# V of two units at once by seven block products, from the second head group on

## The chip, the cores and the metric

The kernel runs on one core of a Trainium2 chip. The metric is the device time in microseconds (us) of one execution. Before the change its median over 3 runs is 834.77 us, from 833.03 to 836.32.

## The reference

A gated cross attention with 32 heads of 128 and then a feed-forward layer with a router and eight low-rank experts, both with a residual. There are 8 batches of 128 tokens with 512 features, and a context of the same shape. Cut to what matters here:

```python
x = rmsnorm(layernorm(x)) * ln_weight
h_q = x @ w_q.T
h_k = ctx @ w_k.T
h_v = ctx @ w_v.T
score = softmax(where(m, einsum(h_q, h_k) + position_bias, -inf))
attn = einsum(score, h_v)
out = attn @ w_out.T
x = x + tanh(g_xattn) * (hidden + out)
x = x + tanh(g_ffn) * ffn(layernorm(x))
```

Everything is float32. A product is made of three TensorE products of the type fp32r: each operand is split into a rounded part (`_hi`) and the rest (`_lo`), and low x high, high x low and high x high are added up in PSUM.

## The kernel before

Two phases and a tail follow one another.

In the first phase 32 jobs make K and then Q of all heads, two heads a job, and store them to DRAM (`qk_units`). From the third job on a job is done by the Winograd form of Strassen's scheme: seven products of blocks in the place of eight, with four sums of weight blocks (S1 to S4, made by VectorE, DVE) and four sums of context blocks (T1 to T4, kept in `t_hi`, `t_lo`).

In the second phase the heads go in 8 groups of 4. A unit is one batch in one group, so there are 64 units, and `step(g, b, q)` is written for each engine. A step of TensorE (PE) is: `scores` of unit t (4 heads, full float32), the first half of V of unit t+1 (`v_half`), the first half of the output projection of unit t-5 (`out_half`), the second halves of both, and `apply_probs` of unit t-3. V of a unit is 12 matmuls of 512 columns: four chunks of the 512 features by the three parts. ScalarE (ACT) copies V out of PSUM (`v_evict`), makes the high parts of the weights and of the attended values, and does the exponentials. GpSimd (POOL) adds bias and mask and makes the low parts of the weights. DVE adds scores and bias, finds the maxima, normalises, transposes 32x32 blocks and adds the projections to `acc`.

All DMAs are issued by SyncE (SP), in the order in which they are written, and they go through one hardware queue. In a step of group g SP does: `store_blocks` (probabilities to DRAM, `p_rows`), `load_unit` (K and Q of a later unit, 512 KB), `load_blocks` (four DMAs back into `pT`, after a wait for the landing of the rows), then one load of 256 KB of weights for a later step. Groups 1 to 6 are a hardware loop of two groups each; group 0 and group 7 are written out. In group 0 `first_units` has the first steps, and `group(0, 0)` goes on from step 4.

Each engine works through its own list in order and waits on semaphores; no planner moves anything.

Of the kernel before, what the change touches and what calls it, by code (L numbers as in the profile page):

```python
# [50 lines left out]

def build(nc, x, ctxT, mask, g_xattn, g_ffn, bias, lnw, wqk, wv, wo, baseT, base_b, loraR, router_b,
          lora_B, expert_map, qk_units, p_rows, out):
    with ExitStack() as ctx:
# [16 lines left out]
        c_hi, c_lo = sb("c_hi", [P, 4, 2, TH], F32R), sb("c_lo", [P, 4, 2, TH], F32R)  # L71
# [31 lines left out]
        with ExitStack() as first_phase:  # L103
# [3 lines left out]
            t_hi, t_lo = sb_a("t_hi", [P, 4, 2, TH], F32R), sb_a("t_lo", [P, 4, 2, TH], F32R)  # L107
# [15 lines left out]
        v_hi1, (v_raw1, v_lo1) = sb("v_hi1", [P, DC, HU * DH], F32R), loaded_and_low("v1", [P, DC, HU * DH])  # L123
        o_hi1, (o_raw1, o_lo1) = sb("o_hi1", [P, HU, D], F32R), loaded_and_low("o1", [P, HU, D])
        hwT_hi, hwT_lo = (sb(n, [P, BH * S], F32R)[:, :] for n in ("hwT_hi", "hwT_lo"))

        y_cols01 = sb("y_cols01", [P, 2, DC, S])
        v_hi0, (v_raw0, v_lo0) = sb("v_hi0", [P, DC, HU * DH], F32R), loaded_and_low("v0", [P, DC, HU * DH])
# [6 lines left out]
        out_more = sb("out_more", [P, D])  # L135
        y_ring = sb("y_ring", [P, 2, D])
        spare = sb("spare", [P, D])

        p_blocks, pT = sb("p_blocks", [P, 2, Q32, HU, 32]), sb("pT", [P, 4, Q32, HU, 32])
        x_again = sb("x_again", [P, 2, D])  # L140
        A_hi, A_lo = sb("A_hi", [P, 2, HU, S], F32R), sb("A_lo", [P, 2, HU, S], F32R)
        y_cols23 = sb("y_cols23", [P, 2, DC, S])
        y_cols = [t[:, k, :, :] for t in (y_cols01, y_cols23) for k in range(2)]

        v_raw, v_hi, v_lo = [v_raw0, v_raw1], [v_hi0, v_hi1], [v_lo0, v_lo1]
        o_raw, o_hi, o_lo = [o_raw0, o_raw1], [o_hi0, o_hi1], [o_lo0, o_lo1]
        picked = spare[:, 0:BH * E * NR].rearrange("p (i e n) -> p i e n", i=BH, e=E)

        base_raw, w_base_hi, w_base_lo = o_raw0, o_hi0, o_lo0
        loraR_all = v_raw0[:, 0:2, :].rearrange("p c n -> p (c n)")[:, 0:DC * RW].rearrange("p (c n) -> p c n", c=DC)  # L150
        loraB_raw, w_loraB_hi, w_loraB_lo = v_raw0[:, 2, :], v_hi0[:, 2, :], v_lo0[:, 2, :]
# [57 lines left out]
        v_done, v_out = sem("v_done"), sem("v_out")  # L209
        o_done, acc_done = sem("o_done"), sem("acc_done")  # L210
# [46 lines left out]

        def x_columns(t, j):
            b = tok(j % BH)
            return t[:, 0:2, :, b].rearrange("p k c n -> p (k c) n") if j < BH else t[:, 2, :, b]  # L260
# [5 lines left out]
        def c_tile(t, j, c):  # L266
            return t[:, 2 * (j // BH) + c // 2, c % 2, tok(j % BH)]
# [11 lines left out]
        def v_bank(t, b):  # L279
            return V_bank[b % 2]  # L280

# [21 lines left out]
        def _(sp):  # L303
# [15 lines left out]
            def load_wv(g, q, k):  # L319
                if k == 0:  # L320
                    reached(sp, v_done, B * (g - 1))
                sp.dma_start(v_raw[q][:, k, :], wv[g, :, k, :]).then_inc(ld_wv[k], 16)

            def load_wo(g, q, k):
                if k == 0:
                    reached(sp, o_done, B * (g - 1))
                sp.dma_start(o_raw[q][:, k, :], wo[g, :, k, :]).then_inc(ld_o[k], 16)
# [20 lines left out]
            def load_unit(g, b):  # L348
                sp.dma_start(qk[:, b % 4, :, :, :].rearrange("p h a k -> p (h a k)"),
                             qk_units[2 * g + b // BH, :, b % BH, :, :].rearrange("p c k -> p (c k)")).then_inc(  # L350
                                 ld_qk[b % 4], 16)
# [19 lines left out]
            for n in range(JOBS + 1):  # L371
# [5 lines left out]
                if n == 19:  # L377
                    for k in range(4):
                        sp.wait_ge(t_lo_done[k], 2)
                    for k in range(DC):  # L380
                        load_wv(0, 0, k)
                    for k in range(HU):
                        load_wo(0, 0, k)
                if n >= JOBS - 2 and n < JOBS:
                    sp.wait_ge(w2_lo, J(n))
                    sp.wait_ge(st[R11], 16 * (G + 2))
                    sp.wait_ge(st[R21], 16 * (G + 2))
# [15 lines left out]
            def first_units():  # L403
# [18 lines left out]
                for k in range(3):  # L422
                    load_wv(1, 1, k)

            def group(g, q):
                first, last = (isinstance(g, int) and g == n for n in (0, GROUPS - 1))
                for b in range(4 if first else 0, B):
# [3 lines left out]
                    before = (g, b - 1) if b > 0 else (g - 1, B - 1)  # L431
                    store_blocks(*before)
# [14 lines left out]
                    if last and b == 0:  # L447
                        for j in range(2):
                            sp.dma_start(x_again[:, j, :], x[:, j, :]).then_inc(ld_x2[j], 16)
                        sp.wait_ge(v_done, LAST)  # L450
                        sp.dma_start(loraR_all, loraR).then_inc(ld_lora, 16)
                        sp.dma_start(loraB_raw, lora_B).then_inc(ld_loraB, 16)
                    if last and b >= 2:
                        sp.wait_ge(f_u, b - 1)
                        sp.dma_start(x_again[:, b % 2, :], x[:, b, :]).then_inc(ld_x2[b % 2], 16)
# [6 lines left out]
            with sp.Fori(0, GROUPS // 2 - 1) as pair:  # L462
                for k in range(2):
                    group(2 * pair + 1 + k, 1 - k)
# [4 lines left out]
            for j in range(B):  # L469
                sp.wait_ge(f_out, j + 1)  # L470
                sp.dma_start(out[:, j, :], out_ring[j % 2]).then_inc(stored[j % 2], 16)
# [4 lines left out]
        def _(pool):  # L476
# [37 lines left out]
            def split_wv_lo(g, q, k):  # L514
# [1204 lines left out]
```

## Time and profile before

| what | value |
|---|---|
| median of 3 runs | 834.77 us |
| span of the profiled execution, first to last instruction | 830.8 us |
| TensorE busy, weight loads busy | 817.8 us (98%), 695.2 us (84%) |
| DVE, ACT, POOL busy | 59%, 52%, 42% |
| the chain that ended last, on TensorE | 95% |
| first step of group 0 to last step of group 7 | 313 to 763 us |

The page gives no other time of the profiled execution than its span; it lies 4.0 us under the median. A busy time counts an instruction from its start to its modelled end, and matmuls overlap: a matmul of 512 columns is shown as 0.39 us long and the next starts 0.23 us after it. So the pace of TensorE is read from starts and not from lengths. Groups of instructions can mix many places in the program, and a line can be that of a helper (L1339 to L1341 are the three parts of every plain product).

### The profile page before, as it was taken

To read this page: it belongs to the slowest core of one execution; us is meant where nothing else is said; L and a number is where in the kernel's file an instruction comes from. 1 tells how busy PE (TensorE), PEld (TensorE's weight loads), DVE (VectorE), ACT (ScalarE), POOL (GpSimd) and SP (SyncE) were. 2 spreads that over 40 slices of the span, in tenths; PEclk is the share of its full clock that TensorE was granted. 3 is DMA by queue.
4 is the path that set the end of the run, shared out by engine and by line. 5 is a ranking of instruction groups with operands and counts; after the bars stand their busy time and mean duration, and the time that the engine had idled before them with its cause. 6 is when DMAs were issued, how large, how long until landed. Compare 5 with 4: busy or idle time off the path is not lost.

```text
span 830.8 us, 13207 instructions
## 1 busy us (share of the span) xinstructions
PE 817.8 (98%) x4172; PEld 695.2 (84%) x4172; DVE 490.8 (59%) x918; ACT 428.9 (52%) x1064; POOL 348.7 (42%) x223
## 2 busy tenths in 40 slices
PE   6999999999999999999999999999999999999998
PEld 5888888888888888888888888888888888888876
DVE  6666666674353335555665565556655655677875
ACT  6567766676676665544444444444444444444320
POOL 0354544564556551434443344344434434432332
PEclk9999999999999999999999999999999999999999
DMA  8655555568555565766665566676665666654002
GB/s 293 208 168 152 162 164 153 165 178 270 171 168 156 172 202 167 238 193 199 192 209 185 180 197 211 185 202 176 185 194 175 178 192 188 219 164 159 33 26 76
DMA packets 147197, 147.58 MB, mean 178 GB/s; under 512 B 10960, under 2 KB 109392, under 8 KB 146768
## 3 DMA queue, kind: packets, MB, share of 16 engines
q1 hardware_dynamic: 147152, 147.02, 58.3%
q8 instruction: 23, 0.38, 0.2%
q14 instruction: 22, 0.18, 0.1%
HBM read 94.55 MB, written 52.43 MB: 177 GB/s over the span
## 4 chain that ended last, share of the span: by engine, by line
PE 95%; DVE 3%; issue 1%; DMA 0%; ACT 0%; SPq 0%; DVEq 0%
PE Sb L1496 7%; PE Ab L1507 7%; PE Sb L1348 7%; PE Sb L1349 7%; PE Sb L1350 7%; PE Vb L1339 4%; PE Vb L1340 4%; PE Vb L1341 4%; PE Kb L1339 4%; PE Kb L1340 4%; PE Kb L1341 4%; PE Ob L1339 4%; PE Ob L1340 4%; PE Ob L1341 4%; PE Ab L1348 3%; PE Ab L1349 3%
## 5 line engine op out<-in xcount | busy, mean ns | idle before, releaser
L530 POOL TENSOR_TENSOR bm<-bias,maskneg 128x512 f32<-128x512 f32 x64 | 83.7, 1307 | 178.1 <-DVE s_sb L1064 178.1
L750 ACT ACTIVATE p_exp<-s_sb,negmax 128x128 f32<-128x128 f32 x256 | 99.8, 391 | 77.0 <-DVE negmax L1066 77.0
L493 POOL TENSOR_TENSOR w_lo<-w_raw,w_hi 128x1280 fp32r<-128x1280 f32 (+1 forms) x29 | 86.9, 2996 | 117.7 <-ACT w_hi L620 117.7
L620 ACT ACTIVATE A_hi<-Ab 128x512 fp32r<-128x512 f32 x64 | 38.3, 598 | 163.6 <-PE Ab L1507 163.6
L1064 DVE TENSOR_TENSOR s_sb<-Sb,bm 128x512 f32<-128x512 f32 x62 | 42.8, 691 | 122.8 <-PE Sb L1496 122.8
L620 ACT ACTIVATE U<-Sb 128x512 f32<-128x512 f32 x90 | 53.9, 599 | 65.9 <-PE Sb L1350 65.3
L521 POOL TENSOR_TENSOR o_lo<-o_raw,o_hi 128x512 fp32r<-128x512 f32 x32 | 52.5, 1641 | 45.0 <-ACT o_hi L620 45.0
L1507 PEld LDWEIGHTS Ab<-pT,V 128*128 128x128 f32 x512 | 66.9, 191 | 5.0
L620 ACT ACTIVATE w_hi<-w_raw 128x512 fp32r<-128x512 f32 (+2 forms) x67 | 60.0, 900 | 21.2 <-PE Kb L1350 8.5
L1348 PE MATMUL Sb<-t_hi,w_lo 128*128 128x512 f32 x180 | 70.1, 389 | 0.0
L1350 PE MATMUL Sb<-t_hi,w_hi 128*128 128x512 f32 x180 | 70.0, 389 | 0.0
L1349 PE MATMUL Sb<-t_lo,w_hi 128*128 128x512 f32 x180 | 70.0, 389 | 0.0
L516 POOL TENSOR_TENSOR v_lo<-v_raw,v_hi 128x512 fp32r<-128x512 f32 x32 | 51.5, 1612 | 42.2 <-ACT v_hi L620 42.2
L1507 PE MATMUL Ab<-pT,V 128*128 128x128 f32 x512 | 67.3, 274 | 0.0
L1496 PE MATMUL Sb<-qk 128*128 128x128 f32 x496 | 65.5, 275 | 0.0
L1496 PEld LDWEIGHTS Sb<-qk 128*128 128x128 f32 x496 | 60.6, 192 | 0.2
L498 POOL TENSOR_TENSOR w_lo<-w_raw,w_hi 128x512 fp32r<-128x512 f32 x30 | 40.6, 1353 | 37.8 <-ACT w_hi L620 37.7
L1339 PE MATMUL Vb<-v_hi,c_lo 128*128 128x512 f32 x128 | 52.6, 411 | 0.0
L1339 PE MATMUL Kb<-v_hi,c_lo 128*128 128x512 f32 x128 | 52.5, 410 | 0.0
L1087 DVE STREAM_TRANSPOSE p_blocks<-p_norm 128x512 f32<-128x512 f32 x64 | 45.5, 711 | 10.0 <-DVE p_norm L1081 8.3
L1339 PE MATMUL Ob<-o_hi,A_lo 128*128 128x512 f32 x128 | 50.1, 392 | 0.2 <-DVE A_lo L917 0.2
L1340 PE MATMUL Kb<-v_lo,c_hi 128*128 128x512 f32 x128 | 50.0, 391 | 0.0
(276 smaller groups left out, 2090.0 us busy)
## 6 DMA issues: line engine op xcount, KB each, us to landing
qk_units<-unit_out SPq DMA_DIRECT2D x128, 256.0 KB, 2.9
qk<-qk_units SPq DMA_DIRECT2D x64, 512.0 KB, 4.8
p_rows<-p_blocks SPq DMA_DIRECT2D x64, 256.0 KB, 2.7
pT<-p_rows SPq DMA_DIRECT2D x256, 64.0 KB, 2.7
w_raw<-wqk SPq DMA_DIRECT2D x31, 512.0 KB, 4.0
v_raw<-wv SPq DMA_DIRECT2D x32, 256.0 KB, 4.1
o_raw<-wo SPq DMA_DIRECT2D x32, 256.0 KB, 3.9
stage<-ctxT SPq DMA_DIRECT2D x8, 256.0 KB, 5.9
```

Of the source, the lines that this page charges most:

```text
L493: pool.tensor_tensor(w_lo[:, n % 2, first:5, :], w_raw[:, n % 2, first:5, :], f32(w_hi[:, n % 2, first:5, :]), ALU.subtract).then_inc(w1_l ...
L530: pool.tensor_tensor(bm[:, :, :], bias4[:, q, :, :], maskneg[:, b:b + 1, :].broadcast_to([P, HU, S]), ALU.add).then_inc(bm_done, 1)
L620: act.activation(dst, src, ACT.Copy).then_inc(done, 1)
L750: last = act.activation(p_exp[:, i, :], s_sb[:, i, :], ACT.Exp, bias=negmax[:, i:i + 1], accum_out=rowsum[:, i:i + 1])
L1339: pe.matmul(dst, w_lo, m_hi, start=start, stop=False)
L1340: pe.matmul(dst, w_hi, m_lo, start=False, stop=False)
L1341: return pe.matmul(dst, w_hi, m_hi, start=False, stop=stop)
L1348: pe.matmul(bank, lo, m_hi[:, c, :], start=first, stop=False, skip_group_check=not fresh)
L1349: pe.matmul(bank, hi, m_lo[:, c, :], start=False, stop=False, skip_group_check=not fresh)
L1350: last = pe.matmul(bank, hi, m_hi[:, c, :], start=False, stop=c == 1, skip_group_check=not fresh)
L1496: last = pe.matmul(s_bank(u, b)[:, h, :], qk[:, b % 4, h, 1, :], qk[:, b % 4, h, 0, :], start=True, stop=True)
L1507: last = pe.matmul(a_bank(b)[:, h, :].rearrange("p (i r) -> p i r", i=Q32), V[:, b, h, :], pT[:, b % 4, :, h, :], start=True, stop=True)
```

## The change

From group 1 on V is made for two units together, those of batch p and batch p + 4. Their 256 tokens by 512 features, and the 512 x 512 weights of the group, are cut into 2 x 2 blocks (128 tokens, 256 features, 256 columns), and the same Winograd form as in the first phase is used: seven block products, each of 2 chunks by 3 parts = 6 matmuls of 256 columns. So a pair of units takes 42 matmuls of 256 columns, where it took 24 of 512. The sums of context blocks are those of the first phase: SP stores T1 to T4 to DRAM (`ctx_sums`, eight DMAs of 512 KB) in jobs 4 to 7, and reads them back in group 0, since Q's sums overwrite them. Batches go in the order 0, 4, 1, 5, 2, 6, 3, 7. Group 0 makes V as before.

Further parts: ACT takes three copies of 256 columns out of PSUM for a pair and writes one quarter of V; DVE adds the other three quarters, and makes four sums of weight blocks a group; the seven blocks of the weights are split (ACT high, POOL low) in steps 5 to 7 of the group ahead, where four whole chunks were split in steps 3 to 6. The loads of the weights move to steps 2 and 3, two a step, and those of the output weights to step 7 and steps 0 to 2. Group 1 and group 6 are written out, and the loop is one turn shorter.

```diff
-            def v_half(u, g, b, q, k):
+            def v_blocks(dst, i, a, m_hi, m_lo, fresh, done):
+                hi, lo = v_block_hi[a], v_block_lo[a]
+                for c in range(2):
+                    first = fresh and c == 0
+                    pe.matmul(dst, m_lo[:, c, tok(i)], hi[:, c, :], start=first, stop=False, skip_group_check=not fresh)
+                    pe.matmul(dst, m_hi[:, c, tok(i)], lo[:, c, :], start=False, stop=False, skip_group_check=not fresh)
+                    last = pe.matmul(dst, m_hi[:, c, tok(i)], hi[:, c, :], start=False, stop=c == 1,
+                                     skip_group_check=not fresh)
+                last.then_inc(done, 1)
...
+            def vm6(g, i):
+                v_split_reached(g, i, 1)
+                if isinstance(g, int) and g == 1 and i == 0:
+                    pe.wait_ge(ld_t[T2], SUM_LOADED)
+                pe.wait_ge(vu_done, 3 * v_job(g, i) + 1)
+                v_blocks(VX, i, S2, t_hi[:, T2, :, :], t_lo[:, T2, :, :], False, vm_done[6])
...
+            def v_part(g, b, k):
+                first, last = (isinstance(g, int) and g == n for n in (0, GROUPS - 1))
+                job = (g + 1, 0) if b == B - 1 else (g, (b + 1) // 2)
+                ends = last and b == B - 1
+                if first and b < B - 1:
+                    v_half(b + 1, k)
+                elif b % 2 == 1 and k == 0:
+                    if not ends:
+                        vm1(*job)
+                    if not first:
+                        vm3(g, b // 2)
+                elif b % 2 == 1:
+                    if not ends:
+                        vm6(*job)
+                        vm2(*job)
+                elif k == 0:
+                    vm7(*job)
+                    vm5(*job)
+                else:
+                    vm4(*job)
...
                 if not (first and b < 5):
                     out_half(*before, 1)
+                if first and b == B - 1:
+                    for k in (T3, T1, T4):
+                        pe.wait_ge(ld_t[k], SUM_LOADED)
                 apply_probs(t - 3, *((g, b - 3) if b >= 3 else (g - 1, b + 5)))
...
+            def load_context_sum(k):
+                for part, t in enumerate((t_hi, t_lo)):
+                    sp.dma_start(f32(t[:, k, :, :]), ctx_sums[k, part, :, :, :]).then_inc(ld_t[k], 16)
...
-                for k in range(3):
-                    load_wv(1, 1, k)
+                for k in (RAW_A21, RAW_A22, RAW_A11, RAW_A12):
+                    load_wv(1, k)
+                load_context_sum(T2)
...
-                    if 1 <= b <= 4 and not last:
-                        load_wv(g + 1, 1 - q, b - 1)
-                    if b >= 5 and not last:
-                        load_wo(g + 1, 1 - q, b - 5)
-                    if b == 0:
-                        load_wo(g, q, 3)
+                    if 2 <= b <= 3 and not first and not last:
+                        for k in ((RAW_A21, RAW_A22), (RAW_A11, RAW_A12))[b - 2]:
+                            load_wv(g + 1, k)
+                    if first and b < 7:
+                        load_context_sum((T3, T1, T4)[b - 4])
+                    if b == 7 and not last:
+                        load_wo(g + 1, 1 - q, 0)
+                    if b < 3 and not first:
+                        load_wo(g, q, b + 1)
```

The first place is TensorE in the last step of group 0, where the second half of V follows the first half of the output projection (`Vb`, `Kb`, `Ob`, `Ab`, `Sb` are PSUM banks). Before:

```order
L1339 MATMUL Ob<-o_hi0,A_lo 128x512
L1340 MATMUL Ob<-o0_lo,A_hi 128x512
L1341 MATMUL Ob<-o_hi0,A_hi 128x512
L1339 MATMUL Vb<-v_hi1,c_lo 128x512
L1340 MATMUL Vb<-v1_lo,c_hi 128x512
L1341 MATMUL Vb<-v_hi1,c_hi 128x512
```

Now, with the first product that reads a loaded context sum (`ld_xA` is the semaphore of T2's loads, `vu_done` that of ACT's copies):

```order
L1541 MATMUL Ob<-o_hi0,A_lo 128x512
L1542 MATMUL Ob<-o0_lo,A_hi 128x512
L1543 MATMUL Ob<-o_hi0,A_hi 128x512
L1669 MATMUL Vb<-va_hi,t_lo 128x256 [waits vu_done,ld_xA,w2_lo]
L1670 MATMUL Vb<-va_lo,t_hi 128x256
L1671 MATMUL Vb<-va_hi,t_hi 128x256
```

Matmuls of 256 columns stand in the place of those of 512, and the product waits for ACT and for a load. The end of the same step in the changed kernel, and the beginning of group 1 (`ld_xB`, `ld_w0a` and `ld_w0b` are the semaphores of T3, T1 and T4):

```order
L1541 MATMUL Ob<-o_hi0,A_lo 128x512
L1542 MATMUL Ob<-o0_lo,A_hi 128x512
L1543 MATMUL Ob<-o_hi0,A_hi 128x512
L1790 MATMUL Ab<-pT,V 128x128 [waits pt_done0,v_out,ld_w0b,a_lo_done,ld_w0a,ld_xB]
L1790 MATMUL Ab<-pT,V 128x128 x3
L1775 MATMUL Sb<-qk 128x128 [waits s_done,ld_qk0]
L1775 MATMUL Sb<-qk 128x128 x3
L1669 MATMUL Vb<-v_hi0,t_lo 128x256 [waits vu_done,w2_lo]
```

`apply_probs` of this one step stands behind the landing of three context sums; before, it waited for its probabilities, V and a buffer alone.

The second place is SP in group 0, from the weights of group 1 on. Before:

```order
L322 DMA v_raw<-wv 128x512 [waits m4_done]
L322 DMA v_raw<-wv 128x512 x2
L335 DMA p_rows<-p_blocks 128x512 [waits blocks_done,pt_done1]
L349 DMA qk<-qk_units 128x1024 [waits scores_done]
L341 DMA pT<-p_rows 32x4x128 [waits rows_done]
L341 DMA pT<-p_rows 32x4x128 x3
L322 DMA v_raw<-wv 128x512
L346 DMA bias<-bias 128x512
```

Now:

```order
L403 DMA v_raw<-wv 128x512 [waits m4_done]
L403 DMA v_raw<-wv 128x512 x3
L417 DMA t_hi<-ctx_sums 128x1024
L417 DMA t_lo<-ctx_sums 128x1024
L425 DMA p_rows<-p_blocks 128x512 [waits blocks_done,pt_done1]
L440 DMA qk<-qk_units 128x1024 [waits scores_done]
L431 DMA pT<-p_rows 32x4x128 [waits rows_done]
L431 DMA pT<-p_rows 32x4x128 x3
L417 DMA t_hi<-ctx_sums 128x1024
L417 DMA t_lo<-ctx_sums 128x1024
L436 DMA bias4<-bias 128x512
```

One more load of weights and the two parts of T2 stand ahead of the rows of step 4, and the two parts of T3 stand in the place of one load of weights; in steps 5 and 6 T1 and T4 stand in the same way where a load of output weights (L327) stood.

## Rows read from the trace of the kernel before

**Rows 1.** The page: span, busy time of each engine, the chain by engine.
```profile
span 830.8 us, 13207 instructions
PE 817.8 (98%) x4172; PEld 695.2 (84%) x4172; DVE 490.8 (59%) x918; ACT 428.9 (52%) x1064; POOL 348.7 (42%) x223
PE 95%; DVE 3%; issue 1%; DMA 0%; ACT 0%; SPq 0%; DVEq 0%
```

**Rows 2.** Windows, second phase: busy us (x instructions) by engine; clock; DMA share, GB/s.
```profile
500.00:550.00 50.00, 50.00 (x279) 43.48 (x278) 29.59 (x56) 22.57 (x77) 20.57 (x14) 1.00 0.63 190
```

**Rows 3.** Timeline of TensorE, one step: start, length (us), line, out<-in, count.
```profile
502.11 1.06 PE L1496 MATMUL Sb<-qk 128*128 128x128 f32 x8
...
503.24 0.40 PE L1340 MATMUL Vb<-v_lo,c_hi 128*128 128x512 f32 x1
...
508.23 0.39 PE L1341 MATMUL Ob<-o_hi,A_hi 128*128 128x512 f32 x1
508.46 1.05 PE L1507 MATMUL Ab<-pT,V 128*128 128x128 f32 x8
509.35 1.06 PE L1496 MATMUL Sb<-qk 128*128 128x128 f32 x8
```

**Rows 4.** Timeline of all engines, same step: weight loads (PEld) where V begins.
```profile
502.89 0.19 PEld L1339 LDWEIGHTS Vb<-v_hi,c_lo 128*128 128x128 f32 x1
...
503.01 0.19 PEld L1340 LDWEIGHTS Vb<-v_lo,c_hi 128*128 128x128 f32 x1
```

**Rows 5.** Timeline of TensorE in the tail: eight full float32 matmuls of 144 columns.
```profile
780.99 1.15 PE L1532 MATMUL Sb<-v_raw,y_cols 128*128 128x144 f32 x8
...
782.21 0.40 PE L1340 MATMUL Ob<-o_lo,A_hi 128*128 128x512 f32 x1
```

**Rows 6.** Timeline of TensorE at the start, after its longest idle time.
```profile
6.85 0.77 PE L1339 MATMUL Sb<-c_hi,w_lo 128*128 128x512 f32 x1 [6.85 <-DVE c_lo L917]
...
7.84 0.63 PE L1341 MATMUL Sb<-c_hi,w_hi 128*128 128x512 f32 x1
8.27 0.63 PE L1339 MATMUL Sb<-c_hi,w_lo 128*128 128x512 f32 x1
...
10.06 0.39 PE L1340 MATMUL Sb<-c_lo,w_hi 128*128 128x512 f32 x1
```

**Rows 7.** Timeline of SP in group 0: issue time, length of issuing, line, DMA, count.
```profile
336.62 0.43 SPq L349 DMA_DIRECT2D qk<-qk_units  x1
...
338.57 0.38 SPq L335 DMA_DIRECT2D p_rows<-p_blocks  x1
...
344.41 1.92 SPq L341 DMA_DIRECT2D pT<-p_rows  x4
346.37 0.43 SPq L322 DMA_DIRECT2D v_raw<-wv  x1
...
353.34 1.75 SPq L341 DMA_DIRECT2D pT<-p_rows  x4
355.13 0.43 SPq L327 DMA_DIRECT2D o_raw<-wo  x1
...
360.08 1.74 SPq L341 DMA_DIRECT2D pT<-p_rows  x4
361.86 0.43 SPq L327 DMA_DIRECT2D o_raw<-wo  x1
```

**Rows 8.** Windows of 2 us in group 0, columns as in Rows 2: DMA at its fullest.
```profile
328.00:330.00 2.00, 2.00 (x15) 1.79 (x14) 0.44 (x1) 1.49 (x6) 1.09 (x1) 1.00 0.98 268
350.00:352.00 2.00, 2.00 (x16) 1.83 (x15) 0.67 (x1) 1.60 (x3) 0.92 (x1) 1.00 1.10 377
```

**Rows 9.** DMA issues of the whole run: KB of one, median us from issue to landing.
```profile
o_raw<-baseT SPq DMA_DIRECT2D x1, 1024.0 KB, 6.2
```

**Rows 10.** Timeline of TensorE: `apply_probs` that ends the last step of group 0.
```profile
363.66 1.05 PE L1507 MATMUL Ab<-pT,V 128*128 128x128 f32 x8
```

**Rows 11.** Groups of the steady stretch (372 to 748 us): busy us, mean ns of one.
```profile
L516 POOL TENSOR_TENSOR v_lo<-v_raw,v_hi 128x512 fp32r<-128x512 f32 x24 | 40.5, 1686 | 39.0 <-ACT v_hi L620 39.0
L620 ACT ACTIVATE v_hi<-v_raw 128x512 fp32r<-128x512 f32 x25 | 15.4, 616 | 0.0
```

More of the change, by code:

```diff
@@ L141, in build @@
         A_hi, A_lo = sb("A_hi", [P, 2, HU, S], F32R), sb("A_lo", [P, 2, HU, S], F32R)
[L142 to L146, printed above, removed]
+        with ExitStack() as tail:
+            w_loraB_hi = tail.enter_context(nc.sbuf_tensor("w_loraB_hi", [P, D], F32R))[:, :]
@@ L256, in J, with y_tiles, v_tile @@
             return n + 1 - PLAIN
+        def y_tiles(t, t2, j):
+            return (t if j < BH else t2)[:, 0:2, :, tok(j % BH)]
+        def v_tile(of, j, c):
+            half, i = j % 2, j // 2
+            return of(2 * half + c // 2)[:, c % 2, tok(i)]
         def x_columns(t, j):
@@ L431, in group @@
                     before = (g, b - 1) if b > 0 else (g - 1, B - 1)
+                    if b == 2 and not first and not last:
+                        sp.wait_ge(v_lo_done, PRODUCTS + 7 * g)
                     store_blocks(*before)
@@ L461, in _ @@
             group(0, 0)
-            with sp.Fori(0, GROUPS // 2 - 1) as pair:
+            group(1, 1)
+            with sp.Fori(0, GROUPS // 2 - 2) as pair:
                 for k in range(2):
-                    group(2 * pair + 1 + k, 1 - k)
+                    group(2 * pair + 2 + k, k)
+            group(GROUPS - 2, 0)
             group(GROUPS - 1, 1)
@@ L587, in _ @@
                 step(0, b, 0)
-            with pool.Fori(0, GROUPS // 2 - 1) as pair:
+            for b in range(B):
+                step(1, b, 1)
+            with pool.Fori(0, GROUPS // 2 - 2) as pair:
                 for k in range(2):
                     for b in range(B):
-                        step(2 * pair + 1 + k, b, 1 - k)
-            for b in range(B):
-                step(GROUPS - 1, b, 1)
+                        step(2 * pair + 2 + k, b, k)
+            for k in range(2):
+                for b in range(B):
+                    step(GROUPS - 2 + k, b, k)
             def base_low(k):
@@ L1130, in step @@
                 first, last = (isinstance(g, int) and g == n for n in (0, GROUPS - 1))
+                job = (g + 1, 0) if b == B - 1 else (g, (b + 1) // 2)
+                strassen = not (first and b < B - 1) and not (last and b == B - 1)
                 if first and b == 6:
@@ L1134, in step @@
                 attention_lo(t - 4, b % 2)
+                if b % 2 == 1 and not first:
+                    v_c12(g, b // 2)
+                if strassen and b % 2 == 0:
+                    v_c22(*job)
+                if not last and b == 7:
+                    weight_sum(g + 1, S4)
                 if last and b >= 6:
@@ L1143, in step @@
                     x1(2)
+                if strassen and b % 2 == 1:
+                    v_c11(*job)
                 normalise(t, b)
                 transpose_blocks(t, b)
+                if not last and 4 <= b <= 5:
+                    for a in ((S1,), (S3, S2))[b - 4]:
+                        weight_sum(g + 1, a)
                 if last and b == 6:
@@ L1238, in _ @@
                 step(0, b, 0)
-            with dve.Fori(0, GROUPS // 2 - 1) as pair:
+            for b in range(B):
+                step(1, b, 1)
+            with dve.Fori(0, GROUPS // 2 - 2) as pair:
                 for k in range(2):
                     for b in range(B):
-                        step(2 * pair + 1 + k, b, 1 - k)
-            for b in range(B):
-                step(GROUPS - 1, b, 1)
+                        step(2 * pair + 2 + k, b, k)
+            for k in range(2):
+                for b in range(B):
+                    step(GROUPS - 2 + k, b, k)
             def logits(h):
@@ L1537, in step @@
                 t = B * g + b
-                first, last = (isinstance(g, int) and g == n for n in (0, GROUPS - 1))
+                first = isinstance(g, int) and g == 0
                 before = (t - 5, g, b - 5, q) if b >= 5 else (t - 5, g - 1, b + 3, 1 - q)
-                after = (t + 1, g, b + 1, q) if b < B - 1 else (t + 1, g + 1, 0, 1 - q)
-                ends = last and b == B - 1
                 scores(t, g, b)
-                if not ends:
-                    v_half(*after, 0)
+                v_part(g, b, 0)
                 if not (first and b < 5):
                     out_half(*before, 0)
-                if not ends:
-                    v_half(*after, 1)
+                v_part(g, b, 1)
                 if not (first and b < 5):
                     out_half(*before, 1)
+                if first and b == B - 1:
+                    for k in (T3, T1, T4):
+                        pe.wait_ge(ld_t[k], SUM_LOADED)
                 apply_probs(t - 3, *((g, b - 3) if b >= 3 else (g - 1, b + 5)))
```

400 lines of the change are left out of this document (285 added, 115 removed).

## Prediction

> **What bounds the kernel now.** I read the page first: the chain that ended last lies on TensorE for 95%, and TensorE is busy for 98% of the span [rows 1]. Then the windows of the second phase: TensorE is busy in all 50 of 50 us there at the clock's upper level (2.4 GHz, granted share 1.00), while DVE has 29.6, ACT 22.6 and POOL 20.6 us of work, and DMA a share of 0.63 [rows 2]. Then the timeline of TensorE for one step: it lasts 509.35 - 502.11 = 7.24 us with no gap in it [rows 3]. So in this phase a column saved on TensorE is time saved, until something else is late. What one matmul costs is read from starts: from 503.24 to 508.23 there are 22 matmuls of 512 columns, 0.2268 us each; a full float32 product of 128 columns shows as two records, and eight of them take 508.46 to 509.35, 0.111 us each [rows 3].
>
> **What is saved on TensorE.** V of a pair of units is 24 x 0.2268 = 5.443 us now, and will be 42 matmuls of 256 columns; 28 pairs change (7 groups of 4). No row shows an fp32r matmul of 256 columns, so its pace is bounded.
> From below: the 128-column float32 records take 0.111 us each, with a weight load for each; 256 columns at 2.4 GHz are 0.1067 us, so each record takes about as long as 256 columns would. Those of 144 columns take (782.21 - 0.227 - 780.99) / 8 = 0.124 us [rows 5], so these records grow with their columns and nothing holds them above that. For fp32r weights, one load starts at 502.89 and the next at 503.01, 0.12 us later [rows 4].
> From above: 512 columns at 2.4 GHz are 0.2133 us, and the matmul takes 0.0135 us more. If that excess belongs to each matmul, 256 columns take 0.1067 + 0.0135 = 0.120 us; if it belongs to the columns, half of 0.2268, 0.113 us. At the lower clock level 512 columns take 8.27 - 7.84 = 0.43 us, which is 512 / 1.2 GHz with no excess [rows 6], so the trace does not tell the two apart.
> I take the middle of the last two, 0.117 us: 42 x 0.117 = 4.914 us a pair, 0.529 us less. **28 x 0.529 = 14.8 us saved**; 11.3 us at 0.120, 19.0 at 0.113, 21.9 at 0.111. The change breaks even on TensorE at 5.443 / 42 = 0.1296 us.
>
> The weight loads grow by 28 x 18 = 504, 0.19 us each as the rows show them, some 96 us on the 695 us that they are busy [rows 1, 4]. The Trainium skill (Perfetto Trace Analysis, Identifying the Most-Contended Engine) takes the busy share of weight loads as the measure of what TensorE has left; by it, 791 us of loads in about 830 would leave almost nothing, and this change would gain little. But the two loads in rows 4 begin 0.12 us apart and are 0.19 us long each: they overlap, and here the measure overstates.
>
> **What it costs: the context sums in group 0.** T1 to T4 come back through SP's one queue, 1024 KB each, between rows that others wait for. SP waits for the landing of a step's probabilities before it goes on. In the trace, the rows issued at 338.57 have landed by 344.41, and those of the next steps by 353.34 and 360.08; the output weights that T4 replaces are issued at 361.86 [rows 7]. I move T4's issue by the bytes put ahead of it. Ahead of the first rows: 256 KB of weights and T2, 1.31 MB. Ahead of the second: T3 for 256 KB of weights (346.37), 0.79 MB more. Ahead of the third: T1 for 256 KB of output weights (355.13), 0.79 MB more. The queue at its fullest moves 377 GB/s, DMA share over 1 [rows 8]: 3.5 + 2.1 + 2.1 = 7.7 us. So T4 is issued at 361.86 + 7.7 = 369.6. A DMA of 1024 KB lands after 6.2 us [rows 9], and T4 is two issues, 0.5 us apart: it lands at 376.3.
> TensorE waits for it before the last `apply_probs` of group 0. That starts at 363.66 now [rows 10]; with 18 matmuls of 256 columns in that step (2.11 us) for 12 of 512 (2.72 us), at 363.05. **So TensorE stands for 13.2 us.** ACT splits the first weight blocks only when V of group 0 is through, which may hold TensorE for some us earlier in this step; that falls into the same wait. After its longest idle time so far, 6.85 us, TensorE ran at the lower level: seven starts from 6.85 to 10.06 took 3.21 us, not 1.59 [rows 6]. I add **1.6 us** for the same after this wait.
> Bounds: at 268 GB/s, which another full window shows [rows 8], the 2.89 MB take 10.8 us, and the wait is 16.3 us. If they delayed nothing, T4 would be issued at 361.86 and the wait would still be 5.5 us.
>
> **What costs nothing, and its cover.** ACT's three copies out of PSUM: each is at most the 0.62 us of 512 columns [rows 11]; M6 follows M1 by half an output projection and, mostly, another product (1.36 + 0.70 us), M7 follows M6 by over 3 us, and M4 follows M7 by 2 us. Without that cover a late copy costs TensorE its lateness, 28 times. DVE gets three adds a pair and four sums a group, each under 0.7 us, on a load of 59% [rows 1]: about 75%. M2 waits for an add that comes some 0.9 us sooner, the tightest of them. POOL's low parts, 1.69 us each [rows 11], stand three, three and one in steps 5 to 7; the first is wanted in step 7, some 7 us after it is done. The output weights now land one step before ACT splits them instead of three; ACT has about 2 us of slack there. The eight stores in jobs 4 to 7 add 1 MB to a job of some 10 us; weights are loaded a job ahead. The order of batches moves nothing in time. The tail has the same products and frees its loads earlier: I count 0.
>
> **The sum.** Against the profiled span: 830.8 - 14.8 + 13.2 + 1.6 = 830.8; the median lies 4.0 us over that span, so 834.8 us.
>
> **Rivals.** *The gain wins (faster).* Matmuls of 256 columns run as the 128-column float32 records do, 0.111 us: 21.9 us saved, 14.8 lost, 827.7 us. For it: nothing in rows 3 to 5 forces more. Against it: the only fp32r row carries an excess of 0.0135 us. The Trainium skill (TensorE: Matmul & The Clock Gate, Back-to-back issue gap) gives 262 cycles for 256 columns, 0.109 us; by it 24.1 us would be saved and the time would be 825.5 us. The trace speaks against its figure for 512 columns, 518 cycles or 0.216 us, with 0.2268 us.
> *T4 does not hold TensorE.* If queue and landings are quicker than the rows suggest, or the wait is covered, 834.8 - 14.8 = 820 us. Against it: even undelayed, T4 lands 5.5 us late.
> *The loads of group 0 cost more than the products save (slower).* Place: the queue of SP from 337 to 380 us. Price: at 268 GB/s 16.3 + 1.6 = 17.9 us; with the excess per matmul, 11.3 us saved: 841.4 us. It decides from 377 us for T4's landing at 0.120 us a matmul, and from 380 us at 0.117. For it: window 328 to 330 is full at 268 GB/s. Against it: the window of the very place shows 377.
> *A new wait in every group.* ACT waits for the output weights, copies late, and TensorE stands 1 us a group: 7 us, 842 us. SP is the engine whose rows come late by some us in places.
> *Weight loads do not overlap for short matmuls.* At 0.19 us each a pair takes 7.98 us, 28 x 2.54 = 71 us more, 920 us. Rows 4 speak against it.
>
> **How the numbers follow.** Forecast 0.42; faster by the matmul's pace 0.27; T4 no hindrance 0.05; slower by the loads 0.18; by a new wait 0.05; by weight loads 0.03. Half a per cent, 4.2 us, is about what a measurement of this kernel can tell from no change. Faster by more: 0.27 + 0.05 = 0.32; within: 0.42; slower: 0.18 + 0.05 + 0.03 = 0.26. The range takes in 827.7 us, somewhat less wait with it, and both slower cases about 842: 825 to 842 us. Outside are T4 without hindrance, the serial loads, and part of the ends, together under 0.2. The forecast's own range is 831 to 839 us.
>
> **What would show it.** In the timeline of the changed kernel, starts of 256-column matmuls in V: 0.117 us apart (over 0.13 and the change loses). A pair of steps: 14.48 us now, 13.95 after. In group 0, an idle time of TensorE of about 13 us ahead of the last `apply_probs`, ended by the DMA of a context sum near 376 us, and starts 0.43 us apart behind it. No other idle time of TensorE between there and the tail. The prediction is wrong if that wait is under 9 us or over 17, or if TensorE stands in every group.

## The result and the profile after

The changed kernel takes **846.61 us** (median of 4 runs, 845.49 to 848.5), the kernel before 835.21 beside it: a ratio of 1.0155, interval 1.0142 to 1.0168. It is slower, above the range of the prediction. The profiled span grew from 830.8 to 843.7 us, by 12.9.

The first lines of the page of the changed kernel (of before: [rows 1]), with its second part's line of the granted clock and the packets of the instruction queue:

```profile
span 843.7 us, 14600 instructions
...
PE 815.0 (97%) x4676; PEld 713.0 (85%) x4676; DVE 568.8 (67%) x1030; ACT 453.5 (54%) x1141; POOL 355.7 (42%) x244
...
PEclk9999999999999999979999999999999999999999
...
q8 instruction: 41, 0.67, 0.3%
...
PE 88%; DVE 6%; issue 3%; ACT 2%; DMA 0%; DVEq 0%; ACTq 0%; SPq 0%
```

In what follows M1 to M7 are the seven block products of a pair of units: M6 multiplies S2 and T2, M7 S3 and T3, and M4 a block of the weights and T4. TensorE has 504 more matmuls and is busy for 2.8 us less, but 28.7 us of the span are now idle (13.0 before), and the chain lies on it for 88%, where it was 95% [rows 1]. The windows tell where (columns as in [rows 2]):

```profile
350.00:400.00 50.00, 39.15 (x248) 35.47 (x247) 29.12 (x50) 20.99 (x67) 19.85 (x16) 0.90 0.76 242
...
500.00:550.00 50.00, 48.75 (x333) 44.51 (x332) 39.89 (x71) 25.97 (x87) 22.15 (x17) 1.00 0.62 187
550.00:600.00 50.00, 47.87 (x320) 44.07 (x320) 34.64 (x63) 21.47 (x73) 14.79 (x12) 0.97 0.59 178
```

Two places stand out by idle time and by a granted clock under 1: the end of group 0, and the stretch around 550 us. Between them a little is missing, as from 500 to 550 us. Before, TensorE was busy in all of each of these ([rows 2] for the second of the three), as two more windows of that kernel show:

```profile
350.00:400.00 50.00, 50.00 (x277) 43.36 (x276) 30.23 (x56) 22.83 (x77) 21.41 (x15) 1.00 0.65 203
...
550.00:600.00 50.00, 50.00 (x279) 43.48 (x278) 30.04 (x55) 22.14 (x76) 20.93 (x14) 1.00 0.63 185
```

The waits of TensorE in the changed kernel from 300 to 400 us (total, times, longest), and the two largest from 395 to 775 us:

```profile
PE Ab L1790 <- issue: 9.0, 1, 9.0
PE Vb L1669 <- ACT VU L726: 1.9, 1, 1.9
```
```profile
PE Sb L1775 <- issue: 2.8, 1, 2.8
PE Vb L1669 <- ACT VU L726: 2.2, 6, 0.4
```

The four, in the order of the kernel:

**Group 0.** The timeline of TensorE around the last `apply_probs` of group 0 [rows 10]:

```profile
362.25 0.36 PE L1669 MATMUL Vb<-va_hi,t_lo 128*128 128x256 f32 x1 [1.86 <-ACT VU L726]
...
374.29 2.05 PE L1790 MATMUL Ab<-pT,V 128*128 128x128 f32 x8 [8.99 <-issue]
376.13 1.91 PE L1775 MATMUL Sb<-qk 128*128 128x128 f32 x8
```

M6 waits 1.9 us for ACT, and `apply_probs` 9.0 us. For the second wait the profile names no releaser ("issue"). It is put down to T4 by SP's timeline (of before: [rows 7]), and experiments 1 and 7 bear that out:

```profile
359.75 0.43 SPq L417 DMA_DIRECT2D t_hi<-ctx_sums  x1
...
368.44 0.43 SPq L417 DMA_DIRECT2D t_hi<-ctx_sums  x1
368.92 0.43 SPq L417 DMA_DIRECT2D t_lo<-ctx_sums  x1
```

T4 is issued at 368.44 and 368.92. Its second part lands 5.2 us after its issue, at 374.1, and TensorE goes on at 374.29, at the clock's lower level: `apply_probs` and the scores behind it show 2.05 and 1.91 us in the place of 1.05.

**The pace of 256 columns.** One stretch of the steady state, TensorE's timeline:

```profile
485.68 0.28 PE L1669 MATMUL Kb<-v_hi,cs_lo 128*128 128x256 f32 x1
...
486.40 0.40 PE L1541 MATMUL Ob<-o_hi,A_lo 128*128 128x512 f32 x1
...
487.78 0.28 PE L1669 MATMUL Vb<-va_hi,t_lo 128*128 128x256 f32 x1
```

Six starts from 485.68 to 486.40 are 0.120 us each. The six of 512 columns behind them take 1.38 us, 0.230 each, where it was 0.2268 [rows 3].

**A wait in six groups.** In step 6 of groups 1 to 6 M7 starts late. The timelines of ACT and of TensorE in group 1:

```profile
421.79 0.63 ACT L726 ACTIVATE va_hi<-v_raw 128x512 fp32r<-128x512 f32 x1 [4.07 <-DVE v_raw L1257]
...
422.85 0.58 ACT L726 ACTIVATE A_hi<-Ab 128x512 fp32r<-128x512 f32 x1
423.32 0.38 ACT L726 ACTIVATE VU<-Vb 128x256 f32<-128x256 f32 x1
```
```profile
423.10 0.39 PE L1543 MATMUL QP<-o_hi1a,A_hi 128*128 128x512 f32 x1
423.75 0.38 PE L1669 MATMUL Vb<-v_hi,t_lo 128*128 128x256 f32 x1 [0.26 <-ACT VU L726]
```

ACT stands 4.07 us before the high part of S2, a sum of weight blocks that DVE makes, and behind it in ACT's list come the copy of the attended values and the copy out of PSUM that M7 needs. M7 starts 0.65 us after the matmul ahead of it, not 0.23.

**The loop's way back.** Group 4 begins with the second turn of the loop:

```profile
548.12 1.05 PE L1790 MATMUL Ab<-pT,V 128*128 128x128 f32 x8
551.97 1.59 PE L1775 MATMUL Sb<-qk 128*128 128x128 f32 x8 [2.80 <-issue]
...
553.58 0.41 PE L1670 MATMUL Vb<-v_lo,t_hi 128*128 128x256 f32 x1
553.79 0.41 PE L1671 MATMUL Vb<-v_hi,t_hi 128*128 128x256 f32 x1
```

Nothing that the profile shows is waited for ("issue"), and the matmuls behind it are 0.21 us apart, the lower clock level.

**The ledger**, from the starts of the steps. Undisturbed, a step with 18 block matmuls lasts 6.71 us and one with 24 lasts 7.43: 14.14 a pair, 14.48 before. Steps 7 to 62 are 29 of the first kind and 27 of the second, 395.2 us, against 56 x 7.24 = 405.4: 10.2 us saved. Lost in the same steps: 13.4 in steps 7 and 8 (19.0 and 7.79 us), 4.2 in step 6 of six groups and behind it, 5.0 in steps 31 and 32 (10.54 and 8.64 us). The second phase begins 0.2 earlier; from step 63 on it takes 0.9 longer, 0.7 of it M3 of the last pair, which was moved there. -10.2 + 22.6 - 0.2 + 0.9 = 13.1; the spans give 12.9.

### The profile page after: what moved, and what is told of

It reads as the page before. It is cut to its first block, busy times and chain, and to the rows that moved or that the text cites. A ratio compares the mean times of both kernels' runs of the same rounds, so it can differ in the third digit from the quotient of the medians.

```text
span 843.7 us, 14600 instructions
## 1 busy us (share of the span) xinstructions
PE 815.0 (97%) x4676; PEld 713.0 (85%) x4676; DVE 568.8 (67%) x1030; ACT 453.5 (54%) x1141; POOL 355.7 (42%) x244
## 4 chain that ended last, share of the span: by engine, by line
PE 88%; DVE 6%; issue 3%; ACT 2%; DMA 0%; DVEq 0%; ACTq 0%; SPq 0%
PE Sb L1550 6%; PE Sb L1552 6%; PE Sb L1551 6%; PE Sb L1775 6%; PE Ab L1790 6%; PE Ob L1541 3%; PE Ob L1542 3%; PE Ob L1543 3%; PE Ab L1552 3%; PE Ab L1550 3%; PE Ab L1551 3%; PE Vb L1669 3%; PE Vb L1670 3%; PE Vb L1671 3%; PE QP L1541 3%
## 5 line engine op out<-in xcount | busy, mean ns | idle before, releaser
L726 ACT ACTIVATE VU<-Vb 128x256 f32<-128x256 f32 x84 | 32.1, 382 | 64.4 <-PE Vb L1671 64.3
L1228 DVE TENSOR_TENSOR p_norm<-p_exp,rscale 128x512 f32<-128x512 f32 x64 | 52.4, 819 | 2.2
L1064 DVE TENSOR_TENSOR A_lo<-Ab,A_hi 128x512 fp32r<-128x512 f32 x64 | 43.6, 681 | 7.1 <-ACT A_hi L726 7.1
L871 ACT ACTIVATION_READ_ACCUMULATOR p_exp<-s_sb,negmax 128x1 f32 x256 | 48.0, 188 | 0.0
L1213 DVE TENSOR_REDUCE negmax<-s_sb 128x4 f32<-128x512 f32 x64 | 43.9, 686 | 2.2
L789 ACT ACTIVATE unit_out<-Ob 128x512 f32<-128x512 f32 x61 | 36.4, 596 | 12.5 <-DVE Ob L1125 8.7
```

The costliest lines, as they stand in the source:

```text
L726: act.activation(dst, src, ACT.Copy).then_inc(done, 1)
L871: last = act.activation(p_exp[:, i, :], s_sb[:, i, :], ACT.Exp, bias=negmax[:, i:i + 1], accum_out=rowsum[:, i:i + 1])
L1228: dve.tensor_tensor(p_norm[:, :, :], p_exp[:, :, :], scale, ALU.mult).then_inc(norm_done, 1)
```

## The experiments

**1. Without the context sums' loads.** The loads are left out, so the first sums of Q's contexts take their place and V is not the reference's.

```diff
-        SUM_LOADED = 16 + 32
+        SUM_LOADED = 16
...
             def load_context_sum(k):
-                for part, t in enumerate((t_hi, t_lo)):
-                    sp.dma_start(f32(t[:, k, :, :]), ctx_sums[k, part, :, :, :]).then_inc(ld_t[k], 16)
+                return
```

> The changed kernel without the eight loads of context sums in group 0; the stores stay. V is then made with the sums of Q that lie in the tiles, so its values are not the reference's; the work on the engines is the same. Theory (the queue of SP in group 0 holds TensorE): the wait of 9.1 us before the last apply_probs of group 0 goes, and the slow starts behind it; the 2.0 us before M6, which ACT causes, stay. 846.6 - 9.1 - 1.3 = 836 us. Rival (ACT's split of the weights, which waits for V of group 0, is the real hold, and the wait only moves): 843 us or more.

Measured: 836.18 us, ratio 1.0018 (1.0002 to 1.0034), 11.4 us under the changed kernel by the ratios (their difference times 834.5 us, as in what follows). The loads cost that much. One wait is left from 300 to 400 us:

```profile
PE Vb L1668 <- ACT VU L725: 1.9, 1, 1.9
```

So M6's wait does not come from the loads. By the code and ACT's order, ACT holds the first weight blocks of group 1 until V of group 0 is through, and M6 waits for a copy behind them.

**2 and 3. The loop written out**, in the changed kernel and in the one before (the same edit, one turn more).

```diff
-            with pe.Fori(0, GROUPS // 2 - 2) as pair:
+            for pair in range(GROUPS // 2 - 2):
...
```

> The changed kernel with all groups written out, no hardware loop. Theory (the loop's one way back costs 3.1 us of instruction fetching in TensorE's queue and 1.9 us of slow starts behind it): 846.6 - 5.0 = 841.6 us, and no idle time of TensorE between step 31 and step 32. Rival (written-out code costs as much, since instructions are fetched all the time): 846.6 us, with waits spread over the groups.

> The kernel before with all groups written out. In its trace no instruction is fetched while the loop runs, and its steps at the loop's two ways back last 7.24 us like all others. Theory (the way back is free as long as the body stays in the fetch buffer, and written-out code is fetched ahead): 835.2 us, no change. Rival (written-out code costs): over 837 us.

Measured: 842.11 us, ratio 1.0094 (1.0073 to 1.0116), for the changed kernel; 834.56 us, 1.0001 (0.9989 to 1.0013), for the one before. The way back costs the new loop some 5 us and the old one nothing.

**4. Half columns alone.** The kernel before, all groups written out, with each matmul of V of 512 columns as two of 256: 768 matmuls more, no block products, no sums, no new waits. Its V is not the reference's.

```diff
-                for c in (2 * k, 2 * k + 1):
-                    made = product(v_bank(u, b), ...)
+                for r in range(2):
+                    cols = slice(2 * DH * r, 2 * DH * (r + 1))
+                    for c in (2 * k, 2 * k + 1):
+                        ... three matmuls into v_bank(u, b)[:, cols]
```

> The kernel before, written out, with each of the 12 matmuls of V of a unit split into two of 256 columns: the same columns, twice the matmuls, and none of the sums, copies and waits of the change. At 0.120 us each V of a unit takes 24 x 0.120 = 2.88 us in the place of 12 x 0.2268 = 2.72, 64 x 0.158 = 10.1 us more than before_written_out: 845 us. If the 512-column matmuls of the output projection also slow down behind short ones, as they do in the changed kernel (0.231 us in the place of 0.227), 64 x 12 x 0.0045 = 3.5 us more: 849 us. If that slowing comes from the other engines' new work, 845 us stays.

Measured: 845.33 us, ratio 1.0127 (1.0104 to 1.015). By the time alone that is the 845 us of an unchanged projection and not the 849 of a slower one; what tells them apart is the pace in its timeline:

```profile
505.69 0.28 PE L1461 MATMUL Kb<-v_lo,c_hi 128*128 128x256 f32 x1
505.81 0.28 PE L1462 MATMUL Kb<-v_hi,c_hi 128*128 128x256 f32 x1
505.94 0.40 PE L1339 MATMUL QP<-o_hi,A_lo 128*128 128x512 f32 x1
506.17 0.40 PE L1340 MATMUL QP<-o_lo,A_hi 128*128 128x512 f32 x1
```

0.12 us again, and 0.23 for the output projection behind them. A step lasts 7.43 us, not 7.24: 12 matmuls more at 0.0133 us are 0.16, the rest goes with the 12 of the projection. So the excess of some 0.013 us belongs to each matmul, at 256 columns as at 512, and the slower projection comes with the short matmuls and not with the block products' adds and copies. Why it is slower stays open.

**5. The same, in the loop.** The kernel before with its loop of three turns, and V's matmuls halved as in 4 (and V as there).

> The kernel before with its loop kept, in which each matmul of V of 512 columns is two of 256 (as in before_half_columns, whose groups are all written out; V's values are not the reference's here either, since the second half's sum begins in the same bank). TensorE's part of the loop grows from 16 x 32 = 512 matmuls to 16 x 44 = 704; in the changed kernel it has 16 x 41 = 656. Theory: the 5 us that the changed kernel loses at its loop's way back come from the size of the loop's body, so this loop of three turns loses them at both of its ways back: 845.3 + 2 x 5 = 855 us, with an idle time of TensorE of some 3 us and slow starts behind it at each. Rival: they come from something else in the changed kernel (its semaphores, another engine's late turn); the ways back stay free, and it takes 845.3 us as with all groups written out.

Measured: 852.11 us, ratio 1.0204 (1.0185 to 1.0223); 6.4 us over the written-out one by the ratios, where 10 were expected and the rival had none. TensorE's waits from 300 to 775 us, and the timeline at the first way back:

```profile
PE Sb L1501 <- issue: 4.8, 2, 2.5
```
```profile
486.73 1.40 PE L1501 MATMUL Sb<-qk 128*128 128x128 f32 x8 [2.25 <-issue]
487.79 0.56 PE L1460 MATMUL Kb<-v_hi,c_lo 128*128 128x256 f32 x1
488.14 0.41 PE L1461 MATMUL Kb<-v_lo,c_hi 128*128 128x256 f32 x1
```

The two steps at each way back last 4.0 and 4.3 us longer than two undisturbed ones, with the same wait and the same slow starts (8.3 us; the second phase of this execution began 1.6 us earlier). So the loss comes with the size of TensorE's part of the loop: free with 512 matmuls, not with 656 or 704. That a larger body must be fetched again fits the instruction queue: 23 packets in the kernel before, 41 after, 44 here. From 475 to 711 us, through both of its ways back, the kernel before fetches none, while the changed one fetches in its second turn too. The fetching itself was not tried, so the reason stays an inference.

**6. The weight sums one step earlier**, in each group that makes block products.

```diff
-                if not last and 4 <= b <= 5:
-                    for a in ((S1,), (S3, S2))[b - 4]:
+                at = 4 if first else 3
+                if not last and at <= b <= at + 1:
+                    for a in ((S1,), (S3, S2))[b - at]:
```

> The changed kernel, with VectorE's three sums of context tiles one step earlier in every group from the second on (S1 in step 3, S3 and S2 in step 4), the first group as it is. Theory: the wait of TensorE before the seventh block product in step 6 of each of the seven groups (0.5 to 0.7 us each) comes from the sum S2 on VectorE by way of ScalarE's copy of its high part, so it goes: steps 14, 22, 30 and so on last 6.71 us, and the time is 846.6 - 4 = 842.5 us. Rival: the wait comes from ScalarE's own queue, whatever the sums do; the steps stay at 7.2 to 7.4 us and the time at 846.6.

Measured: 843.12 us, ratio 1.0102 (1.0082 to 1.0122), 4.4 us lower by the ratios. Every step 6 now lasts 6.71 us, and from 395 to 775 us one wait is left:

```profile
PE Sb L1776 <- issue: 2.9, 1, 2.9
```

**7. Each sum waited for where it is read.** The waits for T3, T1 and T4 leave `apply_probs` and go to M7, M5 and M4 of the first pair.

```diff
-                if first and b == B - 1:
-                    for k in (T3, T1, T4):
-                        pe.wait_ge(ld_t[k], SUM_LOADED)
...
+                if isinstance(g, int) and g == 1 and i == 0:
+                    pe.wait_ge(ld_t[T4], SUM_LOADED)
```

> The changed kernel, in which TensorE waits for T3, T1 and T4 not before the last scores product of the first group but each at the block product that reads it (T3 and T1 in the first half of step 8, T4 in its second). Theory: T4 lands at 374.1 us as before, and the 3.7 us of step 8's work ahead of the product that reads it go in front of the wait: 9.1 us of wait become 5.4, and the time is 846.6 - 4 = 842.6. Rival: TensorE's later steps wait for the same landing by another way, and it stays at 846.

Measured: 844.38 us, ratio 1.0119 (1.01 to 1.0138), 3 us lower by the ratios, where 4 were expected. From 300 to 400 us:

```profile
PE Vb L1669 <- issue: 3.6, 1, 3.6
PE Vb L1669 <- ACT VU L726: 3.3, 2, 1.9
```

9.0 us at one place became 3.6, with another wait of 1.5 us for ACT behind it.

**8. The sums loaded earlier in SP's queue**, and ACT's first three blocks without the wait for V of group 0.

```diff
                 load_blocks(0, 0)
+                sp.wait_ge(m_done[4], J(JOBS - 1))
+                load_context_sum(T2)
...
                 load_blocks(0, 1)
+                load_context_sum(T3)
...
-                    if first and b < 7:
-                        load_context_sum((T3, T1, T4)[b - 4])
+                    if first and b == 4:
+                        load_context_sum(T4)
...
-                    act.wait_ge(v_done, B)
+                    if n >= 3:
+                        act.wait_ge(v_done, B)
```

> The changed kernel with the four context sums of the first group loaded earlier (T2 and T3 right behind the first two block loads of the second phase, T1 behind a load of the V weights, T4 at step 4 instead of 6), and ScalarE's copy of V's high part in the second group without the wait for the first group's last V. Theory: both waits of step 7 (2 us before the sixth product, 9 us before the last scores product) and the slow starts behind them go: step 7 lasts 6.7 to 7.4 us, and the time is 846.6 - 12.5 = 834 us. Rival: the block loads and the weights are pushed back by the same 4 MB, and TensorE stands earlier in the group, for 5 to 10 us: 840 to 846 us.

Measured: 842.37 us, ratio 1.0088 (1.0064 to 1.0112). By the ratios 5.6 us of the 12.5 went, and the time is the rival's. The four runs lie between 839.68 and 847.55 us, and the trace is that of 847.55. From 340 to 400 us:

```profile
PE Vb L1672 <- ACT VU L728: 6.7, 2, 5.5
PE Ab L1793 <- DMA pT<-p_rows: 2.9, 2, 1.7
```

The sums are there. In steps 6 and 7 the probabilities come late, and with them what ACT does in order: 4.1 us of these waits. SP's timeline has the reason:

```profile
347.15 0.64 SPq L417 DMA_DIRECT2D t_lo<-ctx_sums  x1
347.89 0.53 SPq L425 DMA_DIRECT2D p_rows<-p_blocks  x1
...
356.54 1.74 SPq L431 DMA_DIRECT2D pT<-p_rows  x4
```

From the issue of step 4's 256 KB of probabilities until SP goes on with them 8.6 us pass, behind weights and a sum (5.8 before, [rows 7]). The longest wait, 5.5 us in step 9, has another releaser. ACT stands before an output weight, which SP issues at 381.75, and the copy that M6 needs comes behind it; ACT's timeline:

```profile
386.06 0.63 ACT L728 ACTIVATE o_hi1a<-o1a_raw 128x512 fp32r<-128x512 f32 x1 [9.93 <-DMA o1a_raw<-wo]
```

**9. Edits 2, 6 and 8 together.**

> The changed kernel with all groups written out, VectorE's sums one step earlier, and the context sums loaded earlier. Theory: the three costs (12.5 us of the first group, 5 us of the way back of the loop, 4 us of the sums) add up and all go, so that what is left is the gain of the block products at 0.120 us each: 56 steps in pairs of 14.14 us instead of 14.48; 846.6 - 21.5 = 825 us, 1.2% faster than the kernel before. Rival: they cover each other, and one of them stays: 830 to 835 us.

Measured: 833.65 us, ratio 1.0001 (0.9982 to 1.002): no difference from the kernel before, 9 us short of what was expected, and within the rival's 830 to 835 us. From step 10 on every step lasts 6.71 or 7.43 us; steps 6 to 9 lose 10.5 us (13.5 in the trace of 8), 6.9 of it in step 9.

**10. The sums in a second queue.** As 9, but ACT issues the loads, between its own work, and TensorE waits where it reads, as in 7.

```diff
-                    sp.dma_start(f32(t[:, k, :, :]), ctx_sums[k, part, :, :, :]).then_inc(ld_t[k], 16)
+                    act.dma_start(f32(t[:, k, :, :]), ctx_sums[k, part, :, :, :]).then_inc(ld_t[k], 16)
...
+                if first and 4 <= b <= 5:
+                    load_context_sum((T1, T4)[b - 4])
```

> The kernel of all_three, but the four context sums of the first group are not loaded by SyncE's queue: ScalarE issues them on its own queue (T2 and T3 between its copies of the first units, T1 at step 4, T4 at step 5), so that no block store or load stands behind them, and TensorE waits for each at the block product that reads it. Theory: what all_three lost in its steps 6 to 9 (38.6 us where 28 are work) came from the block loads standing behind the sums in one queue; with two queues steps 6 to 9 last 28 to 30 us and the time is 833.7 - 9 = 825 us, 1.1% faster than the kernel before. Rival: it is the DMA engines' throughput that lacks, in whichever queue the sums stand; the block loads land as late as before and the time stays at 832 to 836.

Measured: 831.8 us, ratio 0.9964 (0.9948 to 0.9979). It is faster than the kernel before, though by a third of what was expected: steps 6 to 8 are nearly clean, and step 9 lasts 13.99 us. Two things differ from 9, but there TensorE had no wait for a sum left, so the place of its waits can weigh little. SP's timeline:

```profile
345.21 0.63 SPq L421 DMA_DIRECT2D p_rows<-p_blocks  x1
...
354.15 1.75 SPq L427 DMA_DIRECT2D pT<-p_rows  x4
...
368.82 0.52 SPq L398 DMA_DIRECT2D qk_units<-unit_out  x1
371.85 0.34 SPq L421 DMA_DIRECT2D p_rows<-p_blocks  x1
...
377.17 0.44 SPq L408 DMA_DIRECT2D o1a_raw<-wo  x1
```

Step 4's probabilities still take 8.9 us, though no sum stands ahead of them in SP's queue (8.6 in 9); step 5's take 4.7, where T4 stood ahead of them in 9 and they took 5.9. So the order in the queue is a part of it, and for step 4 the rival, the throughput of the DMA engines, is not ruled out. In step 9 SP is the late one, as in 8 and 9: before step 7's rows it waits for the landing of the last store of units, and an output weight behind them holds ACT.

**11. These stores a step sooner, and that weight ahead of the block loads.**

```diff
-                    if first and b > 3 and b < 7:
-                        store((R22, R21, R12)[b - 4], JOBS - 1)
+                    if first and b < 6:
+                        for i in ((R22, R21), (R12,))[b - 4]:
+                            store(i, JOBS - 1)
...
+                    early_wo = isinstance(g, int) and g == 1 and b == 0
+                    if early_wo:
+                        load_wo(g, q, b + 1)
                     load_blocks(*before)
```

> The kernel of sums_on_act_queue, in which step 9 alone still loses time (14.0 us where 6.7 are work: SyncE stands before step 7's block store until the last unit store has landed, at 371.8 us, and the output weight that ScalarE copies ahead of its attention copy is issued behind that, at 377.2). Here the last unit stores are issued in steps 4 and 5 instead of 4 to 6, and that one output weight ahead of step 0's block loads instead of behind them. Theory: the wait of 4.1 us and the slow starts behind it go, step 9 lasts 6.7 to 7.4 us, and the time is 831.8 - 7 = 825 us, 1% faster than the kernel before. Rival: the stores crowd the sums out in steps 4 and 5, and TensorE waits for a block load in step 6 or 7 instead: 829 to 832.

Measured: **828.36 us, ratio 0.9917** (0.9898 to 0.9936), the fastest of all, under the kernel before by 5.7 us of the medians and 6.9 by the ratio. That lies between the 825 us of the theory and the 829 of its rival. From 340 to 765 us TensorE has two waits left, and the granted clock is 1.00:

```profile
PE Vb L1677 <- ACT VU L722: 1.7, 1, 1.7
PE Ab L1804 <- DMA pT<-p_rows: 0.8, 1, 0.8
```

The first is still the wait for the output weight, in a step 9 of 9.50 us.

## Why the prediction was wrong

It said 834.8 us, and 846.6 was measured. The largest misses are the loop, which it did not price, and the copies that it took to cost nothing. By its own steps:

- **The pace of 256 columns**: the step was right in kind and mis-sized. 0.117 us was the middle of two bounds; the upper one, 0.120, is what came, with the excess on each matmul. That makes 11.3 us of the 14.8: 3.5 lost. The two forms of the excess were known, and a middle between them stands for neither. The Trainium skill (TensorE: Matmul & The Clock Gate, Back-to-back issue gap) has 262 cycles for 256 columns, 0.109 us at 2.4 GHz, as the gap of an isolated matmul. The trace of this stream disagrees, with 0.120.
- **The output projection** was counted as unchanged. Behind short matmuls it runs at 0.230 us and not at 0.2268 (runs of the changed kernel and of 4), some 0.06 us a pair: 1.8 lost. With it, the gain by steps is 28 x 0.34 = 9.5 us.
- **The wait for T4** held: issued at 368.4 (predicted 369.6), landed by 374.1 (376.3). TensorE came to it at 365.3 (363.05), since M6 had waited. TensorE stands 9.0 us there and 1.9 before M6, where 13.2 were predicted and the second place was named, and the slow starts behind it are there. All in all 13.4 us against 14.8. This term and its mechanism are the best part of the prediction; experiment 1 bears it out with 11.4 us, all but M6's share.
- **"What costs nothing"** failed for ACT's copies. The cover of M7, over 3 us, was worked out from what stands between the products on TensorE, not from what stands ahead of the copy in ACT's list: the high part of S2, which waits for DVE's sum. The rival of a new wait in every group had 7 us; 4.2 came, in six groups, by DVE and not by SP's output weights. Four sums a group were priced by DVE's load, 75%, and not by when they are due. Experiment 6 shows it.
- **The weight loads** overlap, as said: 504 more of them raised their busy time from 695.2 to 713.0 us, 0.035 us each. The rule of the Trainium skill (Perfetto Trace Analysis, Identifying the Most-Contended Engine) that was weighed there would have left almost no gain; undisturbed steps did gain 0.34 us a pair.
- **The loop** was not priced at all. The prediction knew that it is one turn shorter, and counted its instructions nowhere. 5 us (experiments 2, 3 and 5).
- **The tail** lost 0.2 for 0 predicted, apart from the 0.7 of the last pair's M3, which the 28 pairs hold already.

3.5 + 1.8 + 4.2 + 5.0 + 0.2 - 1.4 - 0.2 = 13.1 for a miss of 12.9 in the span, which the prediction had put at 830.8. Its statement of what would show it was of use: the starts, the place of the wait and the slow clock could be read off one by one, and "no other idle time" was the line that failed. Of its signs of being wrong, the wait came out at the bound (8.99 us, for 9), and TensorE does stand in six groups.

Experiments 8 to 11 show that sums loaded earlier move the cost to the round trips behind them, and that unit stores and an output weight in SP's list hold TensorE next. That the loads cost by their place in the one queue is shown in part: in a second queue step 5's round trip got shorter and step 4's did not. Of the 20 us between the changed kernel and the last one, the loop is 5, the sums 4, and the rest group 0, if the single effects add up.

## What to carry to other kernels

A saving by shorter matmuls is to be priced with the excess on every matmul, taken from a row, and then the engines behind it are gone through by their lists: what stands ahead of each copy that TensorE waits for, and what that waits for in turn. A larger loop body can stop being free at its way back, with no wait in the profile but "issue"; writing it out tells at once. Loads put into a queue on which a round trip lies can be paid by the round trip. After a change of queue or place, the time of each round trip, from issue to landing, says whether it got shorter.

## What the hardware showed

- fp32r matmuls of 256 columns start 0.120 us apart, of 512 columns 0.2268, so some 0.013 us above columns / 2.4 GHz at either width.
- 512-column matmuls that follow 256-column ones with no gap run at 0.230 to 0.232 us. Not explained.
- The granted clock was at its lower level for a time after idle times of 9.0 us and of 2.8 us alike (0.85 on average from 376 to 384 us, 0.86 from 549 to 561); behind the 1.9 us before M6, in the changed kernel, the starts stay 0.12 us apart.
- A loop of 512 matmuls (and their loads) on TensorE turned back for nothing, one of 656 or 704 for 4 to 5 us, slow clock included.
- DVE's small product of 128 x 4 elements took 536 ns on average (178 before), and 1.03 us where a subtraction of POOL began just ahead of it; the two end together. The timeline of all engines:

```profile
417.80 1.29 POOL L624 TENSOR_TENSOR va_lo<-v_raw,va_hi 128x512 fp32r<-128x512 f32 x1 [2.39 <-ACT va_hi L726]
...
418.08 1.03 DVE L1223 TENSOR_TENSOR rscale<-rinv,valid 128x4 f32<-128x4 f32 x1
```

The same product took 0.16 us where POOL was idle. This one stands in DVE's list ahead of the sum S2 for which ACT waits in group 1. At 0.16 us the sum would have come 0.87 us sooner, an estimate from these rows, and M7 was only 0.42 us late. So the overlap may be the better part of why the sums were late. It was not tried by itself, and its cost to the kernel is open.
